# Gate and bias vectors loaded as rows and transposed on TensorE, and a new order of the first steps, in a four-layer graph network kernel

## What is computed

```python
# layer 0, twice: h = leaky_relu((A_norm @ h @ W_gcn + b_gcn) @ W_mlp + b_mlp), A_norm from summed edge weights
# layer 1, four blocks: conditioned layernorm, attention over the edges (4 heads), relu MLP
# layer 2: three diffusion steps with the 0/1 adjacency
# layer 3, twice: w = einsum('rb,bio->rio', att, basis)   (2 relations, 30 bases of 512x512)
#          gate = sigmoid(x_j @ gate_w[r]); msg = gate * x_j @ w[type]; segment sum + x @ root + bias
```

## Time and profile before

| | |
|---|---|
| median of 3 runs | 980.94 us (980.0 to 982.46) |
| the profiled execution's own time | 985.52 us |
| its span, first to last instruction | 983.8 us |
| mean granted TensorE clock | 0.946 of full speed |
| PE, DVE, ACT, POOL busy | 89%, 56%, 43%, 23% |
| instructions | 14519 |

### The profile page before, as it was taken

How to read it: one execution, slowest core, us unless ns; L and a number is a source line. 1 busy time by engine, 2 the same in 40 slices (tenths; PEclk the granted TensorE clock), 3 DMA queues, 4 the chain that set the end, 5 groups by cost and what they waited for, 6 DMA issues and landing times.

```text
span 983.8 us, 14519 instructions
## 1 busy us (share of the span) xinstructions
PE 874.9 (89%) x4317; PEld 664.9 (68%) x4318; DVE 549.2 (56%) x1224; ACT 425.4 (43%) x699; POOL 223.8 (23%) x246
## 2 busy tenths in 40 slices
PE   5598987998779999899998999989999685899998
PEld 3355555676467869678696786967869453778877
DVE  6678887746755555555655556555565756310110
ACT  4678884324235742357423574235742151221210
POOL 3000007006240224402244022440224143022200
PEclk9889996999889999999999999999999797599799
DMA  7499913533353453634536345263463752020100
GB/s 162 88 253 248 216 40 79 156 113 109 111 130 92 137 117 109 165 92 137 117 108 164 91 136 119 105 163 91 136 153 105 206 134 51 1 86 1 43 11 33
DMA packets 40929, 113.27 MB, mean 115 GB/s; under 512 B 9040, under 2 KB 9552, under 8 KB 33204
## 3 DMA queue, kind: packets, MB, share of 16 engines
q1 hardware_dynamic: 23700, 79.02, 33.9%
q10 hardware_dynamic: 17184, 33.69, 10.0%
HBM read 105.35 MB, written 7.34 MB: 115 GB/s over the span
## 4 chain that ended last, share of the span: by engine, by line
PE 37%; issue 31%; POOL 12%; DVE 9%; DMA 5%; SPq 4%; ACT 2%; DVEq 0%; POOLq 0%; ACTq 0%
PE ring L1605 25%; POOL wl L666 10%; DMA quad<-in_L_gnn_basis 5%; PE ring L1861 5%; PE ring L1706 3%; SPq L469 3%; PE ring L1623 2%; DVE stats L1072 1%; POOL rstd L671 1%; PE mix_ps L1634 1%; PE mix_ps L1724 1%; PE ring L1683 0%; DVE y L1081 0%; DVE mv L1075 0%; ACT C_h L1013 0%
## 5 line engine op out<-in xcount | busy, mean ns | idle before, releaser
L666 POOL TENSOR_TENSOR wl<-wraw,wh 128x512 fp32r<-128x512 f32 x140 | 176.9, 1298 | 389.8 <-ACT wh L729 389.8
L1706 PE MATMUL ring<-ohs,ohd 128*128 128x512 f32 x312 | 82.2, 412 | 8.2 <-DVE ohs L1240 6.5
L671 POOL TENSOR_TENSOR rstd<-ve,half 128x1 f32<-128x1 f32 x52 | 29.5, 570 | 245.3 <-DVE ve L1077 245.3
L1706 PEld LDWEIGHTS ring<-ohs,ohd 128*128 128x128 f32 x312 | 58.1, 195 | 37.3 <-issue 24.4
L1219 DVE SCALAR_TENSOR_TENSOR ohd<-iota,dstT,vals 128x256 fp32r x156 | 69.5, 477 | 15.7 <-PE ring L1706 13.3
L729 ACT ACTIVATE wh<-wraw 128x2048 fp32r<-128x2048 f32 x35 | 66.6, 1905 | 4.9 <-DMA wraw<-in_L_gnn_root 4.9
L1059 DVE TENSOR_TENSOR qk_l<-ring,qk_h 128x512 fp32r<-128x512 f32 x32 | 21.8, 690 | 77.3 <-ACT qk_h L754 77.3
L754 ACT ACTIVATE yT_h<-ring 128x512 fp32r<-128x512 f32 x32 | 19.1, 597 | 101.2 <-PE ring L1623 101.2
L774 ACT ACTIVATE ohs<-iota,minus_srcT 128x512 fp32r<-128x512 f32 x78 | 52.1, 713 | 19.9 <-PE ring L1706 14.5
L1634 PE MATMUL mix_ps<-quad,att_shift 120*32 120x512 f32 x384 | 52.8, 635 | 0.0
L1059 DVE TENSOR_TENSOR PT_l<-ring,PT_h 128x512 fp32r<-128x512 f32 x64 | 39.6, 681 | 19.6 <-ACT PT_h L754 19.6
(11 more groups left out here) (360 smaller groups left out, 2246.0 us busy)
## 6 DMA issues: line engine op xcount, KB each, us to landing
quad<-in_L_gnn_basis SPq DMA_DIRECT2D x60, 960.0 KB, 8.4
wraw<-in_L_gnn_m_w ACTq DMA_DIRECT2D x8, 1024.0 KB, 5.1
mix_scratch<-mixed SPq DMA_DIRECT2D x128, 32.0 KB, 3.8
wraw<-in_L_gnn_wv ACTq DMA_DIRECT2D x4, 1024.0 KB, 5.4
wraw<-in_L_gnn_wq ACTq DMA_DIRECT2D x4, 1024.0 KB, 5.3
wraw<-in_L_gnn_wk ACTq DMA_DIRECT2D x4, 1024.0 KB, 5.8
wraw<-in_L_gnn_wo ACTq DMA_DIRECT2D x4, 1024.0 KB, 5.4
wraw<-mix_scratch ACTq DMA_DIRECT2D x4, 1024.0 KB, 5.6
```

Of the source, the lines that this page charges most:

```text
L666: last = g.tensor_tensor(wl[s][:, k, :], wraw[s][:, k, :], wh[s][:, k, :].bitcast(F32), ALU.subtract)
L671: g.tensor_tensor(rstd[:, t:t + 1], ve[:, t:t + 1], half[:, 0:1], ALU.pow).then_inc(ln_rstd, 1)
L1706: last = te.matmul(ring[:, banks[b], :], ohd[:, s, b, :], ohs[:, s, :], start=False, stop=False)
```

## The change

Five loads of contiguous rows, 4 x 128 numbers each, bring the four gate vectors and the bias into `vec_rows` (20 x 128); one TensorE transpose, placed behind the four ("T", t), puts them as columns into a new ring tile "vecs", from which DVE makes the high and low parts. The second bias load is gone: the column is read twice. On SP the first basis group of set 0 goes ahead of the four `att` loads. On POOL three iotas move to the front with a semaphore of their own (`numbers_ready`), and the clears of `bias_raw` and seven others now wait for `table_ready` 6, which DVE raises with `turn_hit`. `ones_r` is made on ACT instead of DVE. On PE the transposes of `tab` go ahead of the matmuls of `flag`, and DVE takes `tab` before `flag`.

```diff
-        pre = Tiles(["flag", "tab", "rank", "words"], 0, {"tab": 4, "flag": 5, "rank": 6, "words": 5})
+        pre = Tiles(["tab", "flag", "rank", "words"], 0, {"tab": 4, "flag": 5, "rank": 6, "words": 5})
-        n0 = Tiles([("T", t) for t in range(4)] + [("V", 0), ("V", 1), "dinv", ...
+        n0 = Tiles([("T", t) for t in range(4)] + ["vecs", ("V", 0), ("V", 1), "dinv", ...
-        gw = sb("gw", [P, 2, KT, 2])
-        bgc = sb("bgc", [P, KT, 2])
+        vec_rows = sb("vec_rows", [VECS * KT, P], ctx=ec2)
@@ SP
             sp.dma_start(eint[:, 0, :], src_d...).then_inc(edges_loaded, 16)
+            load_pass_group(0, 0)
             for l in range(2):
                 for r in range(2):
                     sp.dma_start(att[0:QUADS * BASES, l, r:r + 1], ...
-            for k in range(GROUPS):
+            for k in range(1, GROUPS):
                 load_pass_group(0, k)
             sp.wait_ge(const_ready, 2)
...
-                    small(gw[:, l, :, r], l3["gate_w"][l][r, :, 0].rearrange("(k p) -> p k", p=P))
-            for r in range(2):
-                small(bgc[:, :, r], l0["b_gcn"][0, :].rearrange("(k p) -> p k", p=P))
+                    small(vec_rows[(l * 2 + r) * KT:(l * 2 + r + 1) * KT, :], l3["gate_w"][l][r, :, 0].rearrange("(k p) -> k p", p=P))
+            small(vec_rows[(VECS - 1) * KT:VECS * KT, :], l0["b_gcn"][0, :].rearrange("(k p) -> k p", p=P))
@@ POOL
+            g.iota(turn_of[:, 0, :], ...)
+            g.iota(turn_no[:], [[0, 1]], base=0, channel_multiplier=1)
+            g.iota(quadno[:], [[0, 1]], base=0, channel_multiplier=1).then_inc(numbers_ready, 1)
             g.memset(first_code[:], float(TURNS))
...
             g.memset(first_code[0:TURNS, 0:1], 0.0).then_inc(unit_step, 1)
+            pool.wait_ge(table_ready, 6)
             for clear in (bias_raw, fw2, cb, craw, braw, minus_low, minus_loww, quarter):
@@ ACT
+            act.wait_ge(const_step, 1)
+            a.activation(ones_r[:], ones[:], ACT.Copy).then_inc(ones_ready, 1)
             act.wait_ge(dst_loaded, 16)
             act.wait_ge(edges_loaded, 48)
             a.activation(efl[:], eint[:], ACT.Copy).then_inc(edges_cast, 1)
@@ DVE
-            dve.wait_ge(unit_step, 2)
-            v.tensor_scalar(turn_no[:], ...).then_inc(unit_step, 1)
-            dve.wait_ge(unit_step, 3)
+            dve.wait_ge(numbers_ready, 1)
+            v.tensor_scalar(turn_no[:], ...).then_inc(numbers_ready, 1)
+            dve.wait_ge(numbers_ready, 2)
             v.tensor_scalar(turn_f[:], turn_no[:], 1.0, None, ALU.mult)
             v.tensor_scalar(last_turn[:], turn_no[:], float(TURNS - 1), None, ALU.is_equal)
-            v.tensor_copy(ones_r[:], ones[:])
-            dve.wait_ge(const_ready, 1)
             v.tensor_scalar(turn_of[:, 1, :], turn_of[:, 0, :], 0.0, None, ALU.is_ge).then_inc(table_ready, 1)
...
             dve.wait_ge(table_ready, 3)
+            dve.wait_ge(const_ready, 1)
             for b in range(HALVES):
                 last = v.tensor_scalar(hit[:, b, :], eblk[:], float(b), None, ALU.is_equal)
...                                     (the two instructions on "flag" go behind the five on "tab")
-                v.tensor_copy(gwh[:], gw[:]).then_inc(sel_step, 1)
-                v.tensor_copy(bgh[:], bgc[:]).then_inc(sel_step, 1)
+                ready(n0, n0.base, "vecs")
+                gates = bank(n0, "vecs")[:, 0:4 * KT].rearrange("p (l r k) -> p l k r", l=2, r=2)
+                bias = bank(n0, "vecs")[:, 4 * KT:5 * KT].unsqueeze(2).broadcast_to([P, KT, 2])
+                v.tensor_copy(gwh[:], gates).then_inc(sel_step, 1)
+                v.tensor_copy(bgh[:], bias).then_inc(sel_step, 1)
                 dve.wait_ge(sel_step, 6)
-                v.tensor_tensor(gwl[:], gw[:], f(gwh[:]), ALU.subtract).then_inc(sel_step, 1)
-                v.tensor_tensor(bgl[:], bgc[:], f(bgh[:]), ALU.subtract).then_inc(sel_step, 1)
+                v.tensor_tensor(gwl[:], gates, f(gwh[:]), ALU.subtract).then_inc(sel_step, 1)
+                v.tensor_tensor(bgl[:], bias, f(bgh[:]), ALU.subtract).then_inc(tile_taken, 1)
+                taken(n0, n0.base, "vecs")
+                dve.drain().then_inc(sel_step, 1)
@@ PE
             pe.wait_ge(const_ready, 1)
+            pe.wait_ge(edges_cast, 1)
+            pe.wait_ge(edges_loaded, 48)
+            transposes(ring[:, pre.bank("tab"), :], [efl[:, 0, :], efl[:, 1, :], efl[:, 2, :], ewt[:]]).then_inc(tile_ready, 1)
             pe.wait_ge(unit_step, 2)
+            pe.wait_ge(ones_ready, 1)
...                                     (the "flag" matmuls; the transposes behind them are gone)
                 transposes(begin(n0, B, ("T", t)), [cols(xn0, t, k) for k in range(KT)]).then_inc(tile_ready, 1)
+            pe.wait_ge(small_loaded, 16 * SMALL)
+            te.transpose(begin(n0, B, "vecs")[:, 0:VECS * KT], vec_rows[:], ident[0:VECS * KT, 0:VECS * KT]).then_inc(tile_ready, 1)
             pe.wait_ge(weight_lo, 1)
```

More of the change, by code:

```diff
@@ L35 @@
 EVICTS = 2
+VECS = 5
 HEADS = 4
@@ L106, in sem @@
             return top.enter_context(nc.semaphore(name))
-        pre = Tiles(["flag", "tab", "rank", "words"], 0, {"tab": 4, "flag": 5, "rank": 6, "words": 5})
+        pre = Tiles(["tab", "flag", "rank", "words"], 0, {"tab": 4, "flag": 5, "rank": 6, "words": 5})
         mid = Tiles(["deg"], pre.end)
-        n0 = Tiles([("T", t) for t in range(4)] + [("V", 0), ("V", 1), "dinv", ("V", 2), ("V", 3), "z1", "c0"]
+        n0 = Tiles([("T", t) for t in range(4)] + ["vecs", ("V", 0), ("V", 1), "dinv", ("V", 2), ("V", 3), "z1", "c0"]
                    + [("Y", t) for t in range(4)] + ["z2"] + [("H", 0, t) for t in range(4)] + [("G", t) for t in range(4)]
@@ L233, in program @@
         words = sb("words", [1, WORDS + 1], I32, ctx=ec2)
-        sb("unused", [P, 768], ctx=ec2)
+        vec_rows = sb("vec_rows", [VECS * KT, P], ctx=ec2)
+        sb("unused", [P, 640], ctx=ec2)
         bias_raw = sb("bias_raw", [P, D], ctx=ec2)
@@ L312, in program @@
         mix_ps = top.enter_context(nc.psum_tensor("mix_ps", [P, D], F32))
+        numbers_ready = sem("numbers_ready")
         const_ready = sem("const_ready")
@@ L329, in program @@
         unit_step = sem("unit_step")
+        ones_ready = sem("ones_ready")
         flags_ready = sem("flags_ready")
@@ L602, in _ @@
             g = nc.gpsimd
+            g.iota(turn_of[:, 0, :], [[-BODY, TURNS]], base=0, channel_multiplier=1, allow_small_or_imprecise_dtypes=True)
+            g.iota(turn_no[:], [[0, 1]], base=0, channel_multiplier=1)
+            g.iota(quadno[:], [[0, 1]], base=0, channel_multiplier=1).then_inc(numbers_ready, 1)
             g.memset(first_code[:], float(TURNS))
@@ L608, in _ @@
             last.then_inc(const_step, 1)
-            g.iota(turn_of[:, 0, :], [[-BODY, TURNS]], base=0, channel_multiplier=1, allow_small_or_imprecise_dtypes=True)
             g.iota(iota[:], [[1, NODES]], base=-CENTRE, channel_multiplier=0, allow_small_or_imprecise_dtypes=True)
@@ L1112, in _ @@
             v.tensor_copy(half_hit[:], tile_hit[:].unsqueeze(2).broadcast_to([P, HALVES, TURNS])).then_inc(table_ready, 1)
[L1113 to L1118, removed]
             dve.wait_ge(whi_ready, 1)
@@ L1126, in _ @@
             v.tensor_tensor(vals[:, :, 3], tab[:, 3 * P:4 * P], vals[:, :, 1], ALU.subtract).then_inc(tile_taken, 1)
+            ready(pre, pre.base, "flag")
+            hits = bank(pre, "flag")
+            v.scalar_tensor_tensor(unit_none[:], hits[:, 4:8:2], 0.0, last_turn[:].broadcast_to([P, 2]), ALU.is_equal, ALU.mult
+                                   ).then_inc(unit_step, 1)
+            dve.wait_ge(unit_step, 3)
+            v.scalar_tensor_tensor(unit_hit[:, 1:3], hits[:, 0:4:2], 1.0, unit_none[:], ALU.min, ALU.max).then_inc(tile_taken, 1)
             ready(pre, pre.base, "rank")
@@ L1130, in _ @@
             v.scalar_tensor_tensor(unit_first[:], rank[:, 2:4], 1.0, first_code[:], ALU.is_equal, ALU.mult).then_inc(tile_taken, 1)
-            dve.wait_ge(unit_step, 5)
+            dve.wait_ge(unit_step, 4)
             for c in range(2):
@@ L1136, in _ @@
                     v.tensor_scalar(unit_code[:], unit_first[:], turn_f[:], None, ALU.add).then_inc(unit_step, 1)
-            dve.wait_ge(unit_step, 6)
+            dve.wait_ge(unit_step, 5)
             v.tensor_tensor(unit_codes[:], unit_code[:].unsqueeze(2).broadcast_to([P, 2, WORD]),
@@ L1659, in _ @@
             last.then_inc(tile_ready, 1)
-            pe.wait_ge(edges_cast, 1)
-            pe.wait_ge(edges_loaded, 48)
-            transposes(ring[:, pre.bank("tab"), :], [efl[:, 0, :], efl[:, 1, :], efl[:, 2, :], ewt[:]]).then_inc(tile_ready, 1)
             taken(pre, pre.base, "flag")
@@ L1670, in _ @@
                 te.matmul(out[:, WORDS:WORDS + 2], unit_hit[:, c + 1:c + 2], ones_r[:, 0:2], start=c == 0, stop=c == 1)
-            pe.wait_ge(unit_step, 7)
+            pe.wait_ge(unit_step, 6)
             for c in range(2):
@@ L2071, in _ @@
```

(2 more changed lines are left out.)

4 lines of the change are left out of this document (1 added, 3 removed).

## The result

The changed kernel takes 970.5 us, the median of four runs from 969.03 to 971.78, beside 981.64 for the kernel before (four runs, 980.0 to 982.46): a ratio of 0.9888, 95% interval 0.9867 to 0.9909. It is faster, by 11.1 us where 17.4 were forecast, and its median lies 1.5 us above the predicted range. The profiled execution took 970.07 us, its span is 968.3 and its mean granted clock 0.956.

What follows compares the result with a forecast made beforehand. The prediction took SP's late issue of basis loads, stuck in slow gate and bias loads, as the bound. Its terms, 3.0 + 10.64 + 2.5 + 1.26 = 17.4 us, took 980.94 to 963.5 us, range 961 to 969.

Steps and rivals of the forecast that it cites:

- The SP queue: SP's gate and bias issues: 19.84 us removed, 2.0 added, 0.1 waiting; group (1, 0) issued 17.7 us earlier.
- The front chain: Steps before PE's first mix: `words` at 11.4, first mix at 12.8; gain 3.0 us, bounds 0.9 and 3.7.
- POOL's lock on DVE: Rival in the front: `att_shift` on POOL holds DVE's `unit_at` 1.5 to 2 us; time 965.3, chance 0.13.
- The wait of 10.64 and the slow clock: PE before and after group (1, 0): the 10.64 us wait goes, and 2.5 us of slow clock (bounds 0 and 2.7).
- The rival by which the lead of DVE and ACT was missing: Unit loop: without PE's wait, eight slots filled ahead are missing; some 4 us return, time 967.5, chance 0.10.
- The failed step: PE's two later DMA waits: stream moves forward 17.7 us, PE 16.1, so both waits go, gaining 1.26 us.
- the DMA stream becomes the bound: Rival: the saturated basis-group stream can't keep its lead, say SP reaches (1, 0) at 28; shift 12, time 969, chance 0.10.
- theory A: Experiments' account: SP's time in the gate loads is the cost; each us saved there moves the stream by a us.
- Behind the pair table: New transpose fits into PE's 1.50 us wait for DVE (else below 0.5 us); `selectors()` adds perhaps 0.2 us on DVE.

Runs made afterwards that it cites:

- e11: Kernel before, with its six number-by-number gate and bias loads put right behind `src`, ahead of `att` and set 0: 972.14 us, ratio 0.99.
- e6: Kernel before, loads still number by number, with all small and conditioning loads moved behind set 3: 970.9 us, ratio 0.9869.
- e3: Changed kernel with the four `att` loads ahead of the first basis group again: 973.53 us, ratio 0.9878.
- e8: Changed kernel with small and conditioning loads and x behind set 3, and the four `att` loads first: 964.84 us, ratio 0.9823.
- e9: Changed kernel with small loads and x behind set 3, layer 0's `att` ahead of set 0, layer 1's behind it, `att_shift` in halves: 964.7 us, ratio 0.9825.
- e1: Kernel before with only the row loads, the transpose and DVE's new source, queues otherwise in old order: 972.84 us, ratio 0.9881.
- e4: Changed kernel with the 1 MB load of x moved from ahead of group (1, 3) to behind set 3's last group: 966.65 us, ratio 0.9829.
- e10: Changed kernel with two basis groups, (0, 0) and (0, 1), ahead of `att`: 972.01 us, ratio 0.9914.
- e5: Changed kernel with all small and conditioning loads moved from ahead of group (1, 0) to behind set 3: 968.74 us, ratio 0.9842.
- e12: Changed kernel with `att` first and the small loads behind set 3, x in its old place: 965.77 us, one run.
- e2: Changed kernel with the six gate and bias loads number by number as before, keeping only the new order: 978.23 us, ratio 0.9938.
- e7: Changed kernel with small and conditioning loads and x all behind set 3: 966.47 us, ratio 0.9829.

## Why the prediction was right in its sign and missed its size

**The SP queue: right.** 19.84 us of issues went and 1.78 came back, where 2.0 was taken; (1, 0) came 19.4 us earlier instead of 17.7, because the small loads behind the gates also stopped stalling. The reason given, the count of runs, was half of it. By e11 a 512-run load costs SP about 0.5 us where the queue is nearly empty: the 19.84 us were 512 runs behind a full one. And (1, 0) did not land 8.0 us after its issue, as it had before from an idle queue, but 12.8 us after it, at 33.9 instead of the 30.7 predicted; PE needed it at 35.80, so this cost nothing. The Trainium skill ("DMA: Bandwidth & Descriptors", the paragraphs on how many engines a DMA uses) says that one descriptor moves one contiguous run of the last dimension, and the trace agrees: the packets under 512 bytes fell from 9040 to 5892, by 3148, where six loads of 512 runs are 3072. The reading that was wrong is that the run count by itself sets the price of the issue; e11 and e6 show that either fewer runs or another place removes it.

**The front chain: `words` better than predicted, the first mix worse.** `words` was copied at 10.26 (11.4 predicted). But `att` had landed for POOL at 11.04 instead of 9.5, in the middle of the bounds given (8.97 to 12.8), and `att_shift` took 2.17 us, so PE stood 2.13 us for it and the first mix came at 14.37 instead of 12.8. Gain 1.6 instead of 3.0. e3 and e8, with `att` ahead of the first basis group, start at 13.16 and 13.17. By the steps under e9, about 1 us of the 3.0 wouldn't have come through in any case. Moving (0, 0) ahead of `att` "changes nothing in the total" was true of the sum of SP's issues only: it made `att` late for PE, and it began the stream 3.75 us earlier, a gain that the prediction has nowhere.

**POOL's lock on DVE: didn't come.** `unit_at` took 0.41 us, twice, as before, and the DVE step on `words` came early. The rows don't show the coincidence that the rival needed: the second `unit_at` ended at 9.44, POOL's clears at 8.39, and `att_shift` began at 11.04. DVE's first three steps on `tab` did run beside the clears, and took 0.28 us each, where they had taken 0.28 to 0.29.

**The wait of 10.64 and the slow clock: right.** Both are gone, and the pair of mix and units behind it took 4.86 us, so nothing of the 2.7 came back there. The rival by which the lead of DVE and ACT was missing took nothing here. It is real, but only 1.0 to 1.2 us, in e1, e6, e9 and e11, and it goes with the start of PE and not with the wait for (1, 0).

**The failed step: "That stream moves forward by 17.7 ... so it has 1.6 us more room and they go too: 1.26."** I moved the stream by the time that SP had saved. It can move only by the time that the DMA engines were idle: 13.0 us by the windows at 20 to 42 us, 3.1 more at the start, and the earlier trace rows show that nothing behind the gap was idle to be filled. The groups that PE waited for came 14.0, 13.3 and then 12.0 us earlier, and PE, itself 15.3 us earlier by the start of pass 2 (72.94 to 57.60), caught up with them. The two waits of 1.26 us did not go but became three of 4.76: 4.8 us of the shortfall against the step's own sum, beside 1.4 of the front. The account at the landmark is then 1.60 + 10.64 + 2.7 - 3.5 = 11.4, where 12.06 was measured. Of the other 0.6, 0.4 lies in pass 0, which lasted 21.82 us before (15.97 to 37.79) and 21.43 after (14.37 to 35.80). This is the rival "the DMA stream becomes the bound", priced at 969 with a chance of 0.10; its mechanism was the right one, but not its trigger: SP wasn't late, the stream was full. That its 969 lies 1.5 us from the measured time is luck. I had the row of the 0.15 share and read it as the sign of a late queue, when it was also the size of what could be won.

That the stream is the bound is shown by e4 (a megabyte taken out of the way: waits 4.76 to 0, landmark 4.1 us earlier, the ratio clear of the change's) and by e10 (PE 5.7 us later: landmark the same). Against theory A stand the change itself, 19.4 us at the issue and 12.06 at the landmark, and e5, 4.5 us more at the issue and 0.9 at the landmark. e6 shows something else, that SP's long issues may stay if no group stands behind them. What the order contributes beside the rows can't be told in the medians: e1 alone gives 0.9881, the whole 0.9888.

**Behind the pair table: right.** The transpose took 0.23 us, just ahead of a wait of 1.34 for DVE that was 1.50 before. `gwh` and `gwl` took 0.17 us each.

**Left open.** The landmarks of single traces of e1, e3 and e6 (135.5 to 137.5) are later than their ratios suggest. All three begin their basis groups at 5.45, 3.75 us later than the changed kernel, but so does e12, and the rate in its execution made up for it; how much of each landmark is the rate, one trace doesn't say. Nor is it known what decides whether PE has its full clock at the products ("V", m).

**A version that beats both.** e8, and e9 with no measurable difference from it, take 0.9823 and 0.9825 of before. From the changed kernel it takes three moves: x and the small loads behind set 3, and `att` first. The first of them alone, e4, brings 0.9829; the other two make the landmark 2.3 us earlier, but in the ratios their part can't be told.

## What to carry to other kernels

When a late transfer is to be moved forward and the DMA engines are saturated behind it, count the gain as at most their idle time in the gap (one minus the share, times the window), not as the time that the issuing queue saves. Then look at what stands in the full stretch and isn't needed there: here the order of the bytes (x behind the last group) was worth another 0.6%, for one line. Here a load of many short runs was dear to issue behind a full queue and cheap ahead of it, so try the place of such a load before its layout.

## What the runs showed of the hardware that was not expected

- Issuing one 512-run load of 2 KB took 0.5 us of SP into a nearly empty queue (e11) and up to 9.96 us behind four groups of 960 KB (the trace of before). A basis load of 960 KB mostly took 0.84 to 0.92 us to issue even in the full stream, with single ones at 1.41 and 1.78 (after) and 2.23 (before).
- A small load waits for the large one ahead of it: the `att` loads, 0.5 KB each, landed 3.1 us after their issue with nothing large ahead (before), 6.0 us behind one basis group (after) and 9.8 us behind two (e10), as medians of the four.
- The rate of the full stream differs between executions of nearly the same work: 231 to 258 GB/s at 45 to 85 us over the fourteen kernels, at a DMA share of 0.97 or more in each. Of the kernels whose PE waits for groups in passes 2 and 3, e1, e3, e5, e6 and e11 spread by 5.9 to 8.3 us over their runs, and e2 by 5.0; of those whose PE doesn't, e4, e7, e8 and e9 by 1.8 to 3.7 us. The changed kernel, with waits, spreads by 2.8, and e10, without, by 4.4, so this is a tendency and no rule.
